# One pair of PSUM banks for logits, two banks for transposed probabilities and two for the small products

## The reference

```python
x = L0_attn_X                                  # [32, 256, 128]
xn = _layernorm(x)
x = x + attention(xn) + experts(xn)

# attention, per sequence: t = 256 rows, h = 16 heads of dq = 64, nb = 10
Q = X @ Wq + bq;  K = X @ Wk;  V = X @ Wv;  R = X @ Wr + br
d = arange(t)[:, None] - arange(t)[None, :]
valid = (d >= 0) & (d < 128)
extra  = einsum('bhtn,ntp->bhtp', R, where(valid, b_nd[:, d], 0))
logits = einsum('bhtd,bhpd->bhtp', Q, K) / sqrt(dq) + where(valid, 0, -1e9) + extra
A = einsum('bhtp,bhpd->bhtd', softmax(logits), V)
out = A @ Wproj + bproj

# experts: the best 2 of 8 by a router, each w2 @ gelu(w1 @ x + b1) + b2, mixed by a softmax
```

## Time and profile before

| what | value |
|---|---|
| time, median of 3 runs | 1775.75 us (1775.34 to 1776.92) |
| time of the profiled execution | 1773.52 us |
| its span, first to last instruction | 1771.7 us |
| PE busy | 1497.9 us, 85% of the span |
| DVE, ACT, POOL busy | 1026.8, 956.8, 804.7 us |
| granted TensorE clock, mean | 0.972 of full speed |
| PE busy, 400 to 500 us (attention) | 88.27 of 100 us |
| PE busy, 880 to 1080 us (experts) | 200.00 of 200 us |
| experts, first to last matmul | some 818 to 1083 us |
| attention, the first and the second half together | some 1350 us |

### The profile page before, as it was taken

The page is one execution under the profiler, slowest core; times in us unless marked ns, Lnnn a source line. Parts: engine busy times, 40 slices in busy tenths (PEclk is TensorE's granted clock), DMA queues, the critical chain, the costliest instruction groups (busy, mean ns, idle before and its releaser), DMA issues.

```text
span 1771.7 us, 43010 instructions
## 1 busy us (share of the span) xinstructions
PE 1497.9 (85%) x11335; PEld 1150.4 (65%) x11335; DVE 1026.8 (58%) x3715; ACT 956.8 (54%) x2864; POOL 804.7 (45%) x1515
## 2 busy tenths in 40 slices
PE   2556888888888888888999998888888888888886
PEld 1224666666666666667999996666666666666665
DVE  4675666666666666663212122676666766766675
ACT  1223566555666666664444453666665665655654
POOL 0323555655555555561000001555665565655554
PEclk8687999999999999999999998999999999999999
DMA  9765554545545554544666665555555555555541
GB/s 282 276 238 149 153 146 145 150 144 150 157 139 145 148 148 139 149 127 132 200 208 200 209 197 165 145 149 137 153 148 144 150 148 139 153 146 150 147 137 48
DMA packets 375831, 283.10 MB, mean 160 GB/s; under 512 B 16634, under 2 KB 349988, under 8 KB 375716
## 3 DMA queue, kind: packets, MB, share of 16 engines
q1 hardware_dynamic: 367524, 265.16, 50.7%
q0 software_dynamic: 8192, 16.79, 3.6%
HBM read 168.57 MB, written 113.26 MB: 159 GB/s over the span
## 4 chain that ended last, share of the span: by engine, by line
PE 61%; DVE 17%; issue 15%; SPq 4%; DMA 1%; DVEq 1%; POOL 0%; ACT 0%; POOLq 0%; ACTq 0%
PE ps L1381 11%; PE ps L1412 9%; PE ps L1317 8%; PE ps L1281 8%; PE ps L1392 7%; PE ps L1282 7%; PE ps L1283 7%; DVE probT L1073 7%; DVE logit L1093 5%; PE ps L1422 2%; DVE low L1093 1%; PE ps L1299 1%; SPq L435 1%; SPq L396 1%; PE ps L1352 1%
## 5 line engine op out<-in xcount | busy, mean ns | idle before, releaser
L792 ACT ACTIVATE prob<-logit,low 128x128 f32<-128x128 f32 (+1 forms) x1024 | 453.7, 444 | 264.0 <-DVE low L1093 260.1
L1093 DVE CUSTOM_DVE_ANT_0 logit<-ps,extra 128x128 f32<-128x128 f32 (+1 forms) x1024 | 306.3, 355 | 313.1 <-issue 237.9
L1381 PE MATMUL ps<-ident,prob 128*128 128x128 f32 x1536 | 265.7, 282 | 166.7 <-DVE probT L1073 145.1
L666 POOL TENSOR_SCALAR prob<-prob,inv 128x128 f32<-128x128 f32 x512 | 188.4, 368 | 437.9 <-DVE inv L1083 436.7
L1073 DVE COPY probT<-ps 128x384 f32<-128x384 f32 x512 | 284.3, 555 | 110.3 <-PE ps L1381 62.9
L1381 PEld LDWEIGHTS ps<-ident,prob 128*128 128x128 f32 x1536 | 165.1, 141 | 261.1 <-issue 200.1
L776 ACT COPY qk<-ps 128x512 f32<-128x512 f32 x256 | 150.0, 586 | 251.0 <-PE ps L1283 249.6
L668 POOL TENSOR_SCALAR prob<-prob,inv 128x256 f32<-128x256 f32 x512 | 241.2, 471 | 0.0
L1392 PE MATMUL ps<-qk 64*128 64x128 f32 (+1 forms) x2048 | 237.2, 350 | 0.0
L1412 PE MATMUL ps<-probT,val 128*64 128x256 f32 (+1 forms) x2048 | 194.7, 332 | 2.7 <-issue 1.4
L792 ACT ACTIVATION_READ_ACCUMULATOR prob<-logit,low 128x1 f32 x1024 | 191.5, 187 | 0.0
(11 more groups left out here) (171 smaller groups left out, 2425.2 us busy)
## 6 DMA issues: line engine op xcount, KB each, us to landing
skew<-gst SPq DMA_DIRECT2D x256, 256.0 KB
extra<-skew SPq DMA_DIRECT2D x128, 512.0 KB, 3.8
extra<-skew SPq DMA_DIRECT2D x128, 256.0 KB, 2.9
w1b<-w_d SPq DMA_DIRECT2D x39, 514.0 KB, 3.5
w2b<-w_d SPq DMA_DIRECT2D x39, 320.0 KB, 3.3
x_place<-zero SPq DMA_DIRECT2D x39, 256.0 KB, 2.8
placed<-x_place SPq DMA_DIRECT2D x39, 256.0 KB, 3.7
y_place<-yrow SPq DMA_DIRECT2D x39, 256.0 KB, 2.2
```

The lines of the kernel that those rows point to most:

```text
L666: nc.gpsimd.tensor_scalar(prob[:, h, 0:P], prob[:, h, 0:P], inv[:, h, 0:1], 1.0, ALU.mult, ALU.mult).then_inc(norm_made, 1)
L792: ins = nc.scalar.activation(prob[:, h % PB, a:b], logit[:, h % LB, a:b], ACT.Exp, scale=-1.0, bias=low[:, h % LB, t:t + 1], accum_out=tot ...
L1093: ins = nc.vector.tensor_tensor_reduce(out=logit[:, h % LB, a:b], in0=ps[:, S_BANK[j % 2][n], a:b], in1=extra[:, h, a:b], scale=1.0, scala ...
L1381: mm = nc.tensor.transpose(ps[:, PT_BANK, n * P:(n + 1) * P], prob[:, h % PB, n * P:(n + 1) * P], ident[:, :])
```

## The change

It gives the banks out anew: logits get one pair (0, 1) instead of two; transposed probabilities get banks 2 and 3 in turn by the head's parity; U and G get banks 6 and 7 in turn by the unit's number. Bank 4 (keys) stays, and V and O keep one bank (5 instead of 6). The waits follow: T waits for the copy of two heads back, a unit for the copy two units back, and L for the L1093 of the pair just before.

```diff
-        S_BANK, KEY_BANK, PT_BANK, HEAD_BANK, MISC_BANK = ((0, 1), (2, 3)), 4, 5, 6, 7
+        S_BANK, PT_BANK, KEY_BANK, HEAD_BANK, MISC_BANK = (0, 1), (2, 3), 4, 5, (6, 7)
...
-                nc.vector.tensor_copy(probT[:, h % 4, :], ps[:, PT_BANK, 0:3 * P]).then_inc(pT_made, 1)
+                nc.vector.tensor_copy(probT[:, h % 4, :], ps[:, PT_BANK[h % 2], 0:3 * P]).then_inc(pT_made, 1)
...
-                                    out=logit[:, h % LB, a:b], in0=ps[:, S_BANK[j % 2][n], a:b], in1=extra[:, h, a:b],
+                                    out=logit[:, h % LB, a:b], in0=ps[:, S_BANK[n], a:b], in1=extra[:, h, a:b],
...
-                    if n > 0:
-                        _, _, kind0, k0, t0, ahead0 = table[n - 1]
+                    if n >= 2:
+                        _, _, kind0, k0, t0, ahead0 = table[n - 2]
                         unit_taken(pe, kind0, k0, t0, i + ahead0)
                     else:
-                        unit_taken(pe, *START[-1], i)
-                    unit(kind, k, t, i + ahead, par if not ahead else 1 - par)
+                        unit_taken(pe, *START[n - 2], i)
+                    unit(MISC_BANK[n % 2], kind, k, t, i + ahead, par if not ahead else 1 - par)
...
-                wait_from(pe, pT_made, i * H + h)
+                wait_from(pe, pT_made, i * H + h - 1)
...
-                wait_from(pe, logit_made, i * PAIRS + pair - 1)
+                wait_from(pe, logit_made, i * PAIRS + pair)
```

More of the change, by code:

```diff
@@ L752, in _, with values, weights, unit @@
             nc.scalar.activation(ex[:, :], m2[:, :], ACT.Exp).then_inc(route_exp, 1)
-            def values(count, seq, half, tile):
+            def values(count, b, seq, half, tile):
                 act.wait_ge(misc_psum, count + 1)
                 wait_from(act, head_psum, (seq - 1) * QUADS + (half + 1) * QUADS // 2)
-                nc.scalar.copy(val[:, tile, half * BANK:(half + 1) * BANK], ps[:, MISC_BANK, :]).then_inc(val_made, 1)
-            def weights(count, seq, k):
+                nc.scalar.copy(val[:, tile, half * BANK:(half + 1) * BANK], ps[:, b, :]).then_inc(val_made, 1)
+            def weights(count, b, seq, k):
                 act.wait_ge(misc_psum, count + 1)
                 wait_from(act, r_made, 2 * seq + (k - 1))
-                nc.scalar.copy(r_raw[:, k, :], ps[0:RS, MISC_BANK, :]).then_inc(r_copied, 1)
-            def unit(count, kind, k, t, seq):
+                nc.scalar.copy(r_raw[:, k, :], ps[0:RS, b, :]).then_inc(r_copied, 1)
+            def unit(count, b, kind, k, t, seq):
                 if kind == "v":
-                    values(count, seq, k, t)
+                    values(count, b, seq, k, t)
                 elif kind == "r":
-                    weights(count, seq, k)
+                    weights(count, b, seq, k)
             def keys(i, pair):
@@ L783, in sequence @@
                     for n, kind, k, t, ahead in units_at(j, 0, more) if heads else []:
-                        unit(len(START) + i * len(UNITS) + n, kind, k, t, i + ahead)
+                        unit(len(START) + i * len(UNITS) + n, MISC_BANK[n % 2], kind, k, t, i + ahead)
                     if heads:
@@ L1050, in _, with positions @@
             dve.wait_ge(w_stored, 32)
-            def positions(count, seq, g, t):
+            def positions(count, b, seq, g, t):
                 dve.wait_ge(misc_psum, count + 1)
                 wait_from(dve, skew_out[t], (seq * GROUPS + g) * 16)
-                nc.vector.tensor_copy(gst[:, t, :], ps[:, MISC_BANK, :]).then_inc(g_made, 1)
+                nc.vector.tensor_copy(gst[:, t, :], ps[:, b, :]).then_inc(g_made, 1)
             def weights(seq, k):
@@ L1105, in sequence @@
                     for n, kind, k, t, ahead in units_at(j, 1, more) if heads else []:
-                        positions(len(START) + i * len(UNITS) + n, i + ahead, k, t)
+                        positions(len(START) + i * len(UNITS) + n, MISC_BANK[n % 2], i + ahead, k, t)
                     if here(i, j - 2, heads, start):
@@ L1168, in _ @@
                     if kind == "g":
-                        positions(s0 * len(UNITS) + n, s0, g, t)
+                        positions(s0 * len(UNITS) + n, MISC_BANK[n % 2], s0, g, t)
                 sequence(s0, s0)
@@ L1333, in _, with unit @@
             pe.wait_ge(basis_in, 3 * PER * 16)
-            def unit(kind, n, tile, seq, par):
+            def unit(b, kind, n, tile, seq, par):
                 x = (xq_hi[:, par, :], xq_lo[:, par, :])
@@ L1340, in unit @@
                     rows, cols = slice(tile * P, (tile + 1) * P), slice(n * BANK, (n + 1) * BANK)
-                    mm = product(ps[:, MISC_BANK, :], ((x[0][:, rows], x[1][:, rows]),
+                    mm = product(ps[:, b, :], ((x[0][:, rows], x[1][:, rows]),
                                                        (wv_hi[:, cols], wv_lo[:, cols])))
@@ L1351, in unit @@
                     a = n % 2 * T + tile * P
-                    mm = nc.tensor.matmul(ps[:, MISC_BANK, :], rT[:, n // 2, a:a + P], basis[:, :],
+                    mm = nc.tensor.matmul(ps[:, b, :], rT[:, n // 2, a:a + P], basis[:, :],
                                           start=True, stop=True)
@@ L1391, in logits @@
                         rows = slice(DQ * n, DQ * n + DQ)
-                        mm = nc.tensor.matmul(ps[:, S_BANK[pair % 2][n], cols], qk[rows, pair % 2, 0, q],
+                        mm = nc.tensor.matmul(ps[:, S_BANK[n], cols], qk[rows, pair % 2, 0, q],
                                               qk[rows, pair % 2, 1, k], start=True, stop=True)
@@ L1449, in _ @@
                 for n, (kind, k, t) in enumerate(START):
-                    if n > 0:
-                        unit_taken(pe, *START[n - 1], s0)
-                    unit(kind, k, t, s0, 0)
+                    if n >= 2:
+                        unit_taken(pe, *START[n - 2], s0)
+                    unit(MISC_BANK[n % 2], kind, k, t, s0, 0)
                 keys(s0, 0, 0)
```

6 lines of the change are left out of this document (3 added, 3 removed).

## The result

| what | before | after |
|---|---|---|
| time, median of 4 runs each | 1775.78 us | 1554.58 us (1552.70 to 1556.78) |
| time of the profiled execution | 1773.52 us | 1553.0 us |
| ratio of the times, 95% interval | | 0.8754 [0.8739, 0.8769] |

The change takes 221 us, 12.5%, off.

What follows compares the result with a forecast made beforehand. TensorE was taken as the bound, idle in attention where T1 waits for T0's copy. Terms 200 + 3 - 3 - 3 = 197 us off 1773.5, plus 2.2 for the median, gave 1579 us; range 1565 to 1630.

Steps and rivals of the forecast that it cites:

- What bounds the kernel: Whole kernel: TensorE bounds it, busy all the time in the experts, but a ninth idle in attention.
- T1's wait goes: Attention slots: T1, writing T0's bank, no longer waits for DVE's copy of T0, which happened 256 times.
- The size of that term: T1 unheld, 0.35 us behind G: 166.7 + 256 x 0.13 = 200 us gained, 167 to 205.
- My 0.76 and 0.64 a slot: Shortening of two neighbouring attention slots once T1 starts 0.35 us behind G: 1.11 - 0.35 and 0.99 - 0.35.
- U and G, "in the loop nothing": Two banks for U and G: nothing in the loop, 3 us (0 to 6) in each half's first sequence.
- Logits, one pair: L waits for L1093 of the pair just before: no cost, with 0.64 us left at the loop's turn.
- Ends of the halves, -3: V follows closely on T1 there and waits for its copy: 4 of 8 T1 not gained, -3 us (0 to -6).
- POOL's chain, -3: Second half: `rT` waits 0.6 us for POOL's `r_hi`, delaying V6 by 0.2 in 15 sequences: -3 us (0 to -15).
- the two deductions of 3: The terms for the ends of the halves and for POOL's chain in the second half, -3 us each.
- V's wait: Rival, attention: DVE's chain late by 1.6 us holds V, 1681; mild, 0.8 late, 1598; chance 0.19 together.
- L's wait: Rival, attention: with one pair of logit banks L waits for L1093 in each slot, 1912 us; chance 0.04.
- The clock: Rival, attention: TensorE's clock falls to the lower level for part of the work, 1769 to 1959 us; chance 0.03.

Runs made afterwards that it cites:

- the order T0, T1, G: Kernel after with both transposes T0 and T1 ahead of G on TensorE, DVE's copies likewise: 1552.78 us, ratio 0.8756.
- the order G, T0, T1: Kernel after with G ahead of both transposes T0 and T1 on TensorE, DVE's order unchanged: 1564.94 us, ratio 0.8828.
- its own run: Kernel after with transposed probabilities back in one bank, so two banks for U and G and one pair for logits: 1765.19 us, ratio 0.9949.
- The dose of 0.165 us: Kernel after with one 128 x 128 memset that computes nothing on DVE in each slot, between the copies of T0 and G: 1557.15 us, ratio 0.8788.

## Why the prediction came out as it did

- **What bounds the kernel, and that T1's wait goes: right.** The group L1381 fell from 166.7 to 0.1 us idle, no wait of its size took its place, TensorE is busy 99.8 and 100 of 100 us.
- **The size of that term: wrong, and this is the step that failed.** I took 0.35 us from G to an unheld T1, by K behind G, with 0.33 as the least. It is 0.32 in the mean of 240 slots, 0.31 in most, while K behind G in slot 0 of sequence 0 is 0.35 in the kernel after:

```profile
157.12 0.50 PE L1352 MATMUL ps<-basis,rT 120*128 120x512 f32 x1
157.47 0.28 PE L1281 MATMUL ps<-xq_hi,wqk_hi 128*128 128x256 f32 x1
```

  So 0.33 was no floor. I had put the distance down to what follows G, and it goes by what stands ahead of it: L here, transposes in the loop. With transposes ahead K too follows after 0.31 (the order T0, T1, G), and with V ahead a transpose takes 0.34 (the order G, T0, T1). That weight loads of transposes are shorter than K's (141 against 192 ns in the mean) therefore doesn't explain it; why the instruction ahead of G counts, no run shows.

  The sum also left out what comes behind T1: K follows after 0.25 us in the mean, where it took 0.29 behind a T1 that had waited. From G to K the mean slot thus falls from 1.12 + 0.29 to 0.32 + 0.25, by 0.84 us, and 0.83 a slot was measured. Added up over starts, G to T1 gives 193 us in 240 slots, T1 to K 9, and the 16 T1 that have no G ahead of them 15: 217 in place of 200. My 0.76 and 0.64 a slot came from the two slots of the earlier trace rows alone, where G to T1 took 1.11 and 0.99; the mean was 1.12. They make 5.6 us a sequence, 179 us in 32, which didn't fit the 200 of the same prediction; 6.62 was measured.
- **U and G, "in the loop nothing": right for the sum, wrong as a reading.** Against the kernel before nothing waits in the loop, so nothing was gained there. But the second bank is what keeps it so: without it 80 us come back. The prediction priced the removal of T1's wait without asking what that wait had covered for U. At the start of the two halves the term was 3 us and is 9 by its own run, 8 by the starts; I had counted only the waits of two U, and put the G copies down to their DMAs; but of the 10.4 us that G waited for them, 4.4 were the bank's.
- **Logits, one pair: right.** No cost alone (1.0001), and one wait of 0.7 us in the change.
- **Ends of the halves, -3: the size near, by luck.** V waits 0.8 to 0.95 us in four places there (700.19, 704.99, 1537.45, 1542.25), 3.4 us, but it waited 2.7 in the kernel before. The rest stands where I had looked for nothing: V once, with L, in the last sequences (1499.17), and O for `headT`, 1.7 us more. By starts, L to V and L to O lose 3.9 us together.
- **POOL's chain, -3: the mechanism right, the cost not yet there.** In the kernel after DVE comes to `rT` exactly when `r_hi` ends. The timeline of a sequence of the second half, as the earlier trace rows:

```profile
1206.54 1.13 DVE L1136 SCALAR_TENSOR_TENSOR acc<-yget,wtop,acc 128x128 f32 x4
...
1215.71 0.60 POOL L641 CAST r_hi<-r_raw 120x512 fp32r<-120x512 f32 x1
1215.77 0.55 DVE L1073 COPY probT<-ps 128x384 f32<-128x384 f32 x1
...
1216.44 0.76 DVE L1064 SCALAR_TENSOR_TENSOR rT<-r_hi,minus_low,r_raw 120x512 fp32r<-120x512 f32 x1
1217.22 0.25 DVE L1093 CUSTOM_DVE_ANT_0 logit<-ps,extra 128x128 f32<-128x128 f32 x1
...
1219.70 0.54 DVE L1073 COPY probT<-ps 128x384 f32<-128x384 f32 x1
```

  `r_hi` ends at 1216.31, the copy of T1 at 1216.32; `rT` has no idle time, and V6 of this sequence starts at 1220.29, 0.05 after its copy. I had let DVE come to `rT` 1.50 us sooner behind `add_rows`; it is 0.91, since `add_rows` itself ends 0.05 before O3 in place of 0.54, later against TensorE. The second half takes 34.63 us a sequence, the first 34.60 (intervals of the shorter kind). The dose of 0.165 us, which is free in the first half, already costs 0.1 to 0.2 here.
- **The sum.** By starts, 217 in place of 200, 8 in place of 3, and -4 in place of the two deductions of 3: 221. The range's low end took 205 for the first term and 6 for the second, so it rested on the same false floor of 0.33.
- **The rivals.** V's wait is the near one, as its chance of 0.19 said: 0.485 us more on DVE in a slot makes 1579.6, twice that 1657, a loss of 103 us that I had put at a DVE 1.6 late. L's wait, for which I had 0.04, is 1.7 us with 0.97 more in the order of the change, and 12.2 us with the same dose in the order T0, T1, G. The clock stays at 1.00 (400 to 500 and 1200 to 1300 us) with two pairs of banks in turn behind each other. The rule of the Trainium skill (TensorE: Matmul & The Clock Gate, "A second HAM failure mode: psum-queue depth-cycling") is not seen in this trace; its banks in turn are here, its pauses between groups hardly, with TensorE busy 99.8 and 100 of 100 us.

## What to carry to other kernels

Of scarce PSUM banks, give the second one to the place where the writer comes back soonest after its own write, and ask with each wait that you remove which other bank it had kept free: here three places had one bank or two, a spare pair was worth nothing at the logits, 139 us at the transposes, and at the units 9 us alone but 80 behind them. Price what follows an unheld instruction by start-to-start distances with the same instructions ahead, averaged over all slots, and when the trace has no such place, let the range go below the nearest other one. A margin read in one stage holds for that stage only: ask for it again wherever another engine joins the chain.

## What was unexpected of the hardware

- Three fp32 transposes of 128 x 128 (start of the first to start of what follows) take 0.25 us behind O, 0.30 behind V; six take 0.58 to 0.63. What follows G, 512 columns, starts 0.31 us after it where G stands behind transposes, a transpose or K alike, and 0.34 where G stands behind V or L, though its record is 0.48 to 0.50 long.
- The second matmul of K comes 0.20 us after the first behind transposes, 0.12 behind G in the order T0, T1, G. A switch between kinds of products can be paid one matmul later, so orders are to be compared over the whole stretch.
- A short wait can leave no idle time in the records where a modelled end covers it: in the run with one bank for units U at 410.26 comes 0.27 us late and its row names none. The rows name 34 us of waiting on G's copy there (6 with two banks), and the time was 80 us longer.
